# Projecting the next batch's v after that batch's first scores, into the bank of the transposes

## What is computed

```python
Q, K, V = (split_heads(x @ W.T) for W in (Wq, Wk, Wv))
scores = jnp.where(causal, Q @ K^T / 4, -inf)           # per batch and head, 256 x 256
x = layernorm(x + (softmax(scores) @ V) @ Wo.T)
x = layernorm(x + ssm(ctx, z=x))                          # scan over 256 steps, 256 channels x 16 states
for e in range(8):                                        # top 2 of 8 experts per row
    out += w_e * ((silu(0.5 * x @ w_gate[e]) * (x @ w_up[e])) @ w_down[e] * 0.25)
x = layernorm(x + out)
```

## Time and profile before

| what | value |
|---|---|
| time, median of 3 runs | 411.48 us (410.95 to 412.12) |
| the profiled execution's own time | 411.99 us |
| its span, first to last instruction | 410.2 us, so 1.8 us lie around it |
| busy share PE, VectorE, ScalarE, GpSimd | 83%, 62%, 51%, 58% |
| mean granted TensorE clock | 0.955 |

### The profile page before, as it was taken

How to read it: one execution, slowest core, us unless ns; L and a number is a source line. 1 busy time by engine, 2 the same in 40 slices (tenths; PEclk the granted TensorE clock), 3 DMA queues, 4 the chain that set the end, 5 groups by cost and what they waited for, 6 DMA issues and landing times.

```text
span 410.2 us, 5831 instructions
## 1 busy us (share of the span) xinstructions
PE 342.3 (83%) x1860; PEld 202.5 (49%) x1860; DVE 255.3 (62%) x442; ACT 208.8 (51%) x488; POOL 236.3 (58%) x223
## 2 busy tenths in 40 slices
PE   7796678778777687887778878999999999999971
PEld 3363335534346344653435433566666666666541
DVE  2999989897998989689898872222222222222234
ACT  4689798687857788849773112212232222222103
POOL 3076888999999968977789214122332233322214
PEclk9999699987989989998998998999999999999996
DMA  7060111430111210293008941011111111111063
GB/s 215 10 109 20 34 53 38 173 99 27 43 62 51 77 54 27 77 303 110 27 26 287 377 157 51 14 38 53 51 39 40 51 53 40 43 47 38 27 218 102
DMA packets 29455, 34.47 MB, mean 84 GB/s; under 512 B 4074, under 2 KB 23826, under 8 KB 29426
## 3 DMA queue, kind: packets, MB, share of 16 engines
q1 hardware_dynamic: 24770, 26.36, 20.3%
q0 software_dynamic: 2208, 6.03, 4.9%
q10 hardware_dynamic: 2448, 1.71, 1.4%
HBM read 28.92 MB, written 5.18 MB: 83 GB/s over the span
## 4 chain that ended last, share of the span: by engine, by line
PE 36%; DVE 5%; ACT 3%; DMA 2%; POOL 2%; issue 2%; DVEq 0%; POOLq 0%; ACTq 0%
PE psS L1649 19%; PE psD L1668 5%; PE psO L1668 5%; PE psD L1659 2%; PE psT L1644 1%; DMA c_rows<-z_out 1%; POOL rstd L500 1%; ACT experts L692 1%; DMA delta<-x_rows,row_in 1%; PE psS L1460 1%; DMA z_out<-delta,row_out 1%; DVE experts L986 1%; DVE u_sb L1160 1%; PE psT L1488 1%; PE psT L1411 0%
## 5 line engine op out<-in xcount | busy, mean ns | idle before, releaser
L1649 PE MATMUL psS<-experts,delta 128*128 x184 | 86.5, 593 | 0.5 <-ACT delta L820 0.5
L511 POOL TENSOR_TENSOR experts<-experts,c_rows 128x1024 f32<-128x1024 f32 x31 | 73.4, 2369 | 17.3 <-DVE experts L986 17.0
L986 DVE TENSOR_TENSOR_SCAN experts<-experts,psD 128x512 f32<-128x512 f32 x64 | 74.3, 1202 | 0.1
L575 POOL DMA_INDIRECT z_out<-delta,row_out x23 | 22.7, 988 | 88.5 <-ACT delta L834 88.5
L1237 DVE COPY u_sb<-psD 128x512 f32<-128x512 f32 x23 | 15.9, 691 | 68.7 <-PE psD L1659 68.7
L692 ACT ACTIVATE experts<-delta,A_sb 128x255 f32<-128x255 f32 x128 | 54.7, 518 | 0.0
L1411 PE MATMUL psT<-ident,probs_at 128*128 128x128 f32 x192 | 32.0, 291 | 24.2 <-ACT probT L730 24.2
L1649 PEld LDWEIGHTS psS<-experts,delta 128*128 128x128 f32 x184 | 33.1, 190 | 24.3 <-issue 23.3
L974 DVE TENSOR_TENSOR psD<-du,psD 128x512 f32<-128x512 f32 x64 | 41.0, 685 | 2.2 <-PE psD L1369 2.2
L1245 DVE TENSOR_TENSOR du<-du,psS 128x512 f32<-128x512 f32 x23 | 15.8, 687 | 37.3 <-PE psS L1649 37.3
L1411 PEld LDWEIGHTS psT<-ident,probs_at 128*128 128x128 f32 x192 | 22.0, 146 | 33.9 <-ACT probT L730 33.2
(11 more groups left out here) (243 smaller groups left out, 588.0 us busy)
## 6 DMA issues: line engine op xcount, KB each, us to landing
c_rows<-c_dram SPq DMA_DIRECT2D x32, 256.0 KB, 3.3
experts<-in_L_ffn_w_gate_dram SPq DMA_DIRECT2D x8, 512.0 KB, 7.1
experts<-in_L_ffn_w_up_dram SPq DMA_DIRECT2D x8, 512.0 KB, 8.1
experts<-in_L_ffn_w_down_dram SPq DMA_DIRECT2D x8, 512.0 KB, 8.8
x_in<-in_x_dram SPq DMA_DIRECT2D x4, 256.0 KB, 4.7
x_rows<-x_sb SPq DMA_DIRECT2D x4, 256.0 KB, 2.2
probs_at<-z_out SPq DMA_DIRECT2D x4, 256.0 KB, 4.8
c_rows<-z_out ACTq DMA_DIRECT2D x4, 256.0 KB, 5.4
```

Of the source, the lines that this page charges most:

```text
L511: pool.tensor_tensor(states[:, g % ST], states[:, g % ST], c_rows[:, g % CR].rearrange("p n (o s) -> p n o s", o=1).broadcast_to([P, 2, HA ...
L986: dve.tensor_tensor_scan(states[:, g % ST, n].rearrange("p h s -> p (h s)"), dA[:, g % DA, n].rearrange("p h s -> p (h s)"), psD[:, n, :], ...
L1649: ins = pe.matmul(psS[:, bank, :], xgT[:, s % 2, k, :], gate_up_of(bass.ds(e, 1), i)[:, k, :], start=(k == 0), stop=(k == FC - 1))
```

## The change

For the batches 1 to 3, v is no longer projected at m = 7 of the batch before, but at m = 0 of its own batch: the first half between the two broadcasts behind the scores, the second half behind the second broadcast and ahead of `add_last`. It goes into psT and not into psS bank 3, and PE first waits until the attention output of the batch before has been copied out of psT. ScalarE's two copies of v stand no more at m = 7, but at m = 0 between the exponentials of the second and of the third head. The first `scores` of these batches don't wait for v_rdy any more; the first transposes of probabilities do, which write psT next. Batch 0 is as it was.

```diff
             def take_v(b):
                 act.wait_ge(v_ps, b + 1)
-                bank = two(psS[:, 3, :])
+                bank = two(psT[:])
...
                         if m < GROUPS:
                             exponentials(G, r)
+                        if m == 0 and b > 0 and r == 1:
+                            take_v(b)
...
                     elif m == 7 and b + 1 < B:
                         take_k(b + 1)
-                        take_v(b + 1)
...
                 if g == 0:
                     pe.wait_ge(q_rdy, 2 * (b + 1))
                     pe.wait_ge(k_rdy, b + 1)
-                    pe.wait_ge(v_rdy, b + 1)
                     if b > 0:
                         pe.wait_ge(res_rdy, b)
+                    else:
+                        pe.wait_ge(v_rdy, 1)
...
                 take_turn(("prob", 3 * G + j))
+                if j == 0 and G % GROUPS == 0:
+                    pe.wait_ge(v_rdy, G // GROUPS + 1)
...
                     if m < GROUPS:
                         broadcast_b(g + 1, 0)
+                        if m == 0 and g > 0:
+                            pe.wait_ge(psT_taken, taken["oT", f])
+                            project_v(b, 0, psT[:])
                         broadcast_b(g + 1, 1)
                     if m == 0 and g > 0:
+                        project_v(b, 1, psT[:])
                         add_last(f)
...
-                    elif m == 7 and more:
-                        project_v(b + 1, 0, psS[:, 3, :])
-                        project_v(b + 1, 1, psS[:, 3, :])
```

## The result

The changed kernel takes 416.89 us in the median of 4 runs (416.02 to 418.44), the kernel before 411.80 in 4 runs beside it (410.95 to 412.39). The ratio is 1.0116, with an interval of 1.0079 to 1.0153. So it is slower, as forecast, but 3.8 us past the forecast of 413.1 and 2.0 past the upper end of the range. Timed twice more beside the kernel before, it took 417.41 and 416.82, where that took 413.5 and 413.2: ratios of 1.0092 and 1.0083, so by the medians a loss between 3.6 and 5.1 us. The profiled execution took 417.54 us, with a span of 415.8 and a mean granted clock of 0.943.

The account below looks back on a forecast made before the run. VectorE's work and waits bound the stage, with ScalarE the path between the first maxima and second scores. Copies of v cost 0.53 us at three boundaries, other parts 0: 411.48 + 1.59 = 413.1 us, range 411.5 to 414.9.

Parts of the forecast that it names:

- v off the front of the scores: At batch boundaries, scores come some 2 us earlier, but the first maxima still stand behind VectorE's scan; gain 0.
- v behind the scores on PE: At m = 0, `add_last` ends some 0.9 us later, still before the last exponential ends; cost 0.
- The copies between the exponentials: On ScalarE at m = 0, two copies delay the last exponential, and so the second maxima, by 0.53 us per boundary.
- Does the 0.53 last?: Behind each boundary, no later wait was found fixed in time, so the 0.53 us delay stands to the end.
- the new gap: PE's idle stretch of 1.9 us between the first scores and the first broadcast, where the longest before was 0.94.
- VectorE's waits for scores sum to about 10.2: Sign of being right: VectorE's waits for scores sum to about 10.2 us, with about 1.0 at m = 1.
- The base: The starting time: the median of the kernel before, 411.48 us, to which 1.59 us was added.
- The rival of the clock in the new gap: PE's clock falls behind the first scores: 0.57 us more per boundary, 1.7 in all, 414.8 us; chance 0.18.
- The cost is covered: A later VectorE wait, likely the logits', takes up what m = 1 loses; time stays 411.5 us; chance 0.20.
- The clock no longer falls at m = 1: The fall at m = 1 stays away: 2.1 us back against 1.59 lost, 411.0 us; chance 0.07.
- 414.9: Upper end of the range, given for copies at 0.65 us or the clock's fall at all three boundaries.

Follow-up runs that it names:

- e_no_copies: The changed kernel without ScalarE's copies of v for batches 1 to 3 and without the wait for them; 413.27 us, ratio 1.0015.
- f_gap_warm: The changed kernel plus eight unused matmuls on PE between the first scores and the broadcast of batches 1 to 3; 416.79 us, ratio 1.0089.
- the third timing: The changed kernel, word for word, timed once more beside the kernel before; 416.82 us, ratio 1.0083.
- b_again: The kernel before, word for word, run once more; 413.47 us, ratio 0.9998.
- g: d_v_in_gap with VectorE's first maxima ahead of the scan and `add_last` moved to m = 1; 413.38 us, ratio 1.0012.
- h: The changed kernel plus two unused matmuls each at m = 3, m = 4 and m = 6; 414.63 us, ratio 1.0046.
- k: The kernel before plus four ScalarE copies from psT into a spare tile between the exponentials of heads 1 and 2; 418.66 us, ratio 1.0136.
- n: The kernel before plus one unused VectorE copy of 448 columns ahead of the first maxima of batches 1 to 3; 416.65 us, ratio 1.0102.
- o: The kernel before plus one unused VectorE copy of 448 columns behind the residual, ahead of the batch's first product; 417.25 us, ratio 1.0133.
- d_v_in_gap: The changed kernel with both halves of v directly behind the first scores and its copies ahead of the first exponential; 413.76 us, ratio 0.9993.

## Why the prediction was right in kind and wrong in size

- *v off the front of the scores, gain 0*: right. The maxima start behind the scan, without a wait.
- *v behind the scores on PE, cost 0*: right. At batch 2 `add_last` ended at 138.13 + 1.88 = 140.01, ahead of the last mask, which waits for ScalarE until 141.07, and e_no_copies, which keeps all of it, costs nothing that could be measured.
- *The copies between the exponentials, 0.53*: right, 0.51 on ScalarE and 0.55 at VectorE's wait. The estimate from the Trainium skill, ScalarE: Activation LUTs, section "What ACT_TABLE_LOAD costs", was 0.61 for two copies, and four would have been 1.22; the runs show 0.51 to 0.55 and 1.04 to 1.10.
- *Does the 0.53 last?* This is the step that failed. "I find nothing fixed in time, and let it stand to the end" took the rest of the kernel to be shifted and otherwise unchanged. It was not: three times 0.55 is 1.65 us, and the loss was 3.6 to 5.1. The kernel ran at a lower mean clock, 0.946 in place of 0.961, which by the fit is worth a further 2.3 us; in the two timelines set side by side VectorE waits 2.07 us more for PE at the end of batch 3. Rows 9 showed that the clock falls in this stage, and the rivals weighed falls at two places only, the new gap and m = 1. What happens to all the other falls when work moves by half a microsecond was not asked.
- *VectorE's waits for scores sum to about 10.2*: wrong, 8.8, for the same reason: the fall of batch 1 moved from m = 2 to the gap.
- *The base*: "for the median it is 411.48 + 1.59" rested on a median of three runs. The kernel before had a median of 411.8 over the 4 runs beside the result and of 412.3 to 413.5 in the four later sets of 11 to 33 runs, so 411.48 was the low end of what it does. Some 0.3 of the miss of 3.8 us is this beside the result, and up to 2 against the later sets.
- *The rival of the clock in the new gap*: it came at one boundary of three, in each traced execution of the changed kernel, and not as a loss: 1.55 at m = 1 was paid back at m = 2. e_no_copies shows that the gap isn't the price, and f_gap_warm agrees. The Trainium skill, TensorE: Matmul & The Clock Gate, section "Why this matters for your kernels", warns of idle gaps between bursts of matmuls that are longer than any that PE has between 34 and 224 us in the profiles before and after. The trace differs: at batch 1 the clock fell in a gap of 1.86 us, and to fill that gap gave nothing back.
- *The cost is covered*: refuted, since VectorE's scan of m = 2 is 0.55 late behind each boundary of the table, and the time at the end is longer and not the same. *The clock no longer falls at m = 1*: refuted, VectorE still waits 1.73 at m = 2 of batch 2, as before.

One bound doesn't follow from the prediction's own terms: 414.9 is neither 411.48 with three copies at 0.65 (413.4) nor with the clock's fall at all three boundaries (414.8). It decides nothing here, since 416.89 is past both together as well (415.1).

**What stays open** is why a delay of 0.3 to 1.1 us lowers the mean clock. At the end of batch 3 the idle stretches of PE ahead of the fall are the same in both kernels (0.68, 1.00 and 0.56 us in the third timing, 0.68, 0.99 and 0.56 in b_again), and the level falls in one and not in the other. The one thing that I see to differ there in PE's timelines is when they come. A rival that these runs leave is the start of the execution: in all three traced executions of the changed kernel the clock fell in the prologue, which put the first scan some 2 us later, and in one of two of the kernel before. The change can't reach there, and the seven traced kernels e, f, g, h, k, n and o, which have v moved or a delay in them, don't have it, so it is likely chance. But for the executions without a trace it can't be told from the rest of the clock. Whether a delay of another length would raise the clock wasn't tried.

## What to carry to other kernels

Ask of every moved instruction whether its new engine is the path just there: two copies that were free at m = 7, and are free again in ScalarE's idle time ahead of the maxima (d_v_in_gap), cost 0.55 us between the exponentials. In a kernel whose granted clock falls here and there, a small delay on the path has a second price: look at the mean clock of every execution, compare kernels at equal clock, and forecast with a range that holds a change of clock. Set a forecast on more than three runs of the kernel before, and read a loss of 1% from more than one pair of profiles: the two executions of the kernel before differ by 2 us ahead of the first scan alone.

## What the runs showed of the hardware that was not expected

- The same program had mean granted clocks of 0.941 to 0.970 from execution to execution, and its times went from 410.4 to 416.4 us; by the fit 0.01 of mean clock was worth about 1.55 us here, less than half of the 4.1 us that 1% of the time would be.
- In the 16 traced executions of all kernels the first scan starts at 34.0 to 34.4 us where the clock was 1.00 over the first 34 us (eight of them), and at 36.0 to 37.3 where it was 0.95 (the other eight).
- A vector copy of 0.29 us, three times in the whole kernel, came with a mean clock lower by 0.020 and 4.3 us.
- Where a fall of the clock came earlier, the later one stayed away: 1.55 and then 0.50 us of waiting in the changed kernel, 1.68 and 0.34 in e_no_copies, where there were 0.47 and 2.4.
